# Three buffers for normalised x1 and a new order of the query part in a one-core transformer layer

## The reference, cut to what matters

```python
# attention (per batch and head)
Phi_Q = jnp.exp(-C_Q / temperature)          # C_Q: squared distances of queries to landmarks
out_unnorm = jnp.einsum('bhnk,bhkd->bhnd', Phi_Q, Y)
norm = jnp.einsum('bhnk,bhko->bhno', Phi_Q, jnp.linalg.solve(W_kernel, Phi_K_sum))
out = out_unnorm / jnp.maximum(norm, 1e-10)
...
x = _layernorm(x + attention @ Wo.T + bo)
# experts
gate_logits = xf @ Wg.T + bg
topk_vals, topk_idx = jax.lax.top_k(gate_logits, TOP_K)
gate_w = jax.nn.softmax(topk_vals, axis=-1)
...
x = _layernorm(x + experts(x))
```

## Time and profile before

| what | value |
|---|---|
| median of 3 runs | 1957.33 us (1950.88 to 1958.08) |
| the profiled execution | 1951.19 us, span 1949.4 us |
| PE busy | 1436.2 us, 74% of the span |
| DVE busy | 1244.2 us, 64% |
| ACT busy | 976.8 us, 50% |
| POOL busy | 854.8 us, 44% |
| mean granted TensorE clock | 0.871 of full speed |

### The profile page before, as it was taken

One profiled execution on the slowest core, in us unless ns is written; L12 is line 12 of the kernel. 1 busy time (PEld: TensorE's weight loads), 2 busy tenths in 40 slices (PEclk: granted clock), 3 DMA queues, 4 the chain that ended last, 5 costly groups with the idle time before them and its releaser, 6 DMA issues.

```text
span 1949.4 us, 47647 instructions
## 1 busy us (share of the span) xinstructions
PE 1436.2 (74%) x17888; PEld 1138.6 (58%) x17888; DVE 1244.2 (64%) x3410; ACT 976.8 (50%) x1699; POOL 854.8 (44%) x937
## 2 busy tenths in 40 slices
PE   4578989989897887777787888776549988894000
PEld 3267778877785555545565555554339888884000
DVE  5768854798534767767766767575646555552765
ACT  2246666766665755555555555554314333332444
POOL 2300000000001465656656566665467777777544
PEclk9689989999999998888879888889759999998555
DMA  2586786767963343434323333332427766664998
GB/s 87 93 175 143 165 191 152 174 159 172 188 145 104 96 132 108 136 107 139 123 97 112 107 112 117 111 109 91 138 85 221 224 205 212 207 213 133 362 373 298
DMA packets 255998, 307.83 MB, mean 158 GB/s; under 512 B 64896, under 2 KB 187008, under 8 KB 255360
## 3 DMA queue, kind: packets, MB, share of 16 engines
q1 hardware_dynamic: 230240, 234.49, 45.1%
q0 software_dynamic: 25536, 70.31, 9.9%
HBM read 150.02 MB, written 96.50 MB: 126 GB/s over the span
## 4 chain that ended last, share of the span: by engine, by line
PE 23%; DVE 21%; POOL 21%; issue 14%; DMA 12%; SPq 4%; ACT 3%; DVEq 0%; POOLq 0%; ACTq 0%
POOL rows_dram L658 10%; POOL terms_dram L677 6%; DMA rows_dram<-x,place_i 4%; PE bank L346 4%; PE bank L347 3%; PE bank L348 3%; POOL attn_l L642 3%; PE bank L1619 3%; DMA out<-phi 2%; PE bank L1635 2%; DVE st L1285 2%; DVE x L1277 2%; PE bank L1620 2%; DMA tile_in<-terms_dram 2%; DVE inversion L1109 2%
## 5 line engine op out<-in xcount | busy, mean ns | idle before, releaser
L658 POOL DMA_INDIRECT rows_dram<-x,place_i x256 | 283.0, 1106 | 181.3 <-DVE place_i L1346 117.2
L635 POOL TENSOR_TENSOR xl<-x_raw,xh 128x512 fp32r<-128x512 f32 x60 | 75.7, 1288 | 548.9 <-ACT xh L892 548.3
L745 ACT ACTIVATE phi<-bank,invt 128x512 f32<-128x512 f32 x256 | 162.5, 684 | 104.5 <-PE bank L1620 104.3
L868 ACT ACTIVATE phi<-bank,nlt,invt 128x512 f32<-128x512 f32 x256 | 181.3, 776 | 49.2 <-PE bank L1780 46.9
L346 PE MATMUL bank<-weh,kh 128*128 x528 | 161.9, 307 | 29.0 <-DVE kl L1429 28.7
L1619 PE MATMUL bank<-l_hh,k_hl 128*128 128x256 f32 x512 | 145.0, 315 | 40.7 <-DMA k_hl<-kl 27.1
L1429 DVE TENSOR_TENSOR kl<-bank,kh 128x512 fp32r<-128x512 f32 x132 | 90.9, 689 | 126.8 <-ACT kh L941 125.5
L1081 DVE TENSOR_SCALAR phi<-phi,phi_max,phi_min 128x1024 f32<-128x1024 f32 x128 | 103.7, 810 | 102.7 <-ACT phi L745 102.5
L1234 DVE TENSOR_SCALAR phi<-phi,phi_max,phi_min 128x1024 f32<-128x1024 f32 x128 | 111.9, 913 | 84.0 <-ACT phi L868 83.7
L346 PE MATMUL bank<-xh,wh 128*128 128x512 f32 x260 | 120.4, 463 | 51.6 <-DVE x L1277 36.4
L348 PE MATMUL bank<-wel,kh 128*128 x528 | 149.7, 284 | 0.0
(11 more groups left out here) (262 smaller groups left out, 4550.9 us busy)
## 6 DMA issues: line engine op xcount, KB each, us to landing
tile_in<-rows_dram SPq DMA_DIRECT2D x264, 130.0 KB
x_raw<-in_xT SPq DMA_DIRECT2D x64, 512.0 KB, 4.0
x_tok<-in_x SPq DMA_DIRECT2D x32, 512.0 KB, 4.8
attn<-den_dram SPq DMA_DIRECT2D x64, 256.0 KB
phi<-terms_dram SPq DMA_DIRECT2D x22, 512.0 KB, 5.6
out<-phi SPq DMA_DIRECT2D x22, 512.0 KB, 7.7
tile_in<-terms_dram SPq DMA_DIRECT2D x17, 512.0 KB, 7.0
k_hl<-attn_h SPq DMA_DIRECT2D x32, 256.0 KB
```

The source lines that it names most:

```text
L658: nc.gpsimd.indirect_dma_start(out=rows_dram, out_offset=bass.IndirectOffsetOnAxis(ap=place_i[:, at:at + 1].bitcast(u32), axis=0), in_=x1[ ...
L745: nc.scalar.activation(phi[:, n], bank[6 + s][:], ACT.Exp, scale=invt[:]).then_inc(exp_done, 1)
L868: nc.scalar.activation(phi[:, i], bank[4 + i % 4][:], ACT.Exp, bias=nlt[:, c // CPB, i:i + 1], scale=invt[:]).then_inc(qexp_done, 1)
```

## The change

Buffers: x1 gets three buffers, `place_i` two. The second set of query halves (`q_h1`, `q_l1`) no longer has memory of its own; it lies where the key and value projections' weights lay (`wh[:, 0:2]`, `wl[:, 0:2]`), which the query part does not read. The waits on `scattered` reach one chunk further back. Order: the calls in the loops of all five engines stand in another order, partly with another chunk index.

```diff
-FIRST_WEIGHTS = 2
+FIRST_WEIGHTS, X1 = 2, 3
...
-        x1 = [sb(f"x1_{i}", [P, TPC, ROW]) for i in range(2)]
+        x1 = [sb(f"x1_{i}", [P, TPC, ROW]) for i in range(X1)]
-                                 sb("place_i", [P, 2 * TPC], i32))
+                                 sb("place_i", [P, 2, 2 * TPC], i32))
-        q_h, q_l, q_sq = ([kh[0], sb("q_h1", [P, KC, CH], f32r)], [kl[0], sb("q_l1", [P, KC, CH], f32r)],
-                          [sq, sb("q_sq1", [P, KC, CH])])
+        used_up = [a[:, 0:2].rearrange("p w k n -> p (w k n)").rearrange("p (k n) -> p k n", k=KC) for a in (wh, wl)]
+        q_h, q_l, q_sq = [kh[0], used_up[0]], [kl[0], used_up[1]], [sq, sb("q_sq1", [P, KC, CH])]
```

SyncE:

```diff
-                if a - 1 > 0:
-                    load_rows(a - 1)
+                store_inverses(a + 1)
+                spread_inverses(a + 1)
+                if n > 0:
+                    load_query_x(n + 2)
+                if a + 1 > 0:
+                    load_rows(a + 1)
...
-                store_inverses(a)
-                spread_inverses(a)
-                if n - 1 > 0:
-                    load_query_x(n + 1)
```

GpSimd:

```diff
-                attn_lo(a - 1, 0)
-                attn_lo(a - 1, 1)
-                scatter(p - 1, 2)
-                scatter(p - 1, 3)
-                if n - 1 > 0:
-                    split_lo(n, 1)
-                ln1(c)
-                scatter(p, 0)
-                scatter(p, 1)
+                scatter(p, 2)
+                if n > 0:
+                    split_lo(n + 1, 1)
+                ln1(c + 1)
+                scatter(p, 3)
+                scatter(p + 1, 0)
+                attn_lo(a + 1, 0)
+                attn_lo(a + 1, 1)
+                scatter(p + 1, 1)
```

ScalarE:

```diff
-                save_attention(q - 1, 0)
-                q_exps(q, range(2, 4))
-                save_logits(p)
-                gate_exp(p)
-                q_exps(q, range(4, 6))
-                q_exps(q, range(6, 8))
+                normalise_rows(c, c % X1)
                 queries(n, 0)
-                save_attention(q - 1, 1)
                 queries(n, 1)
                 attn_hi(a, 0)
...
                 x1_copy(p + 1, 0)
                 x1_copy(p + 1, 1)
                 q_exps(q + 1, range(0, 2))
+                save_attention(q, 0)
+                q_exps(q + 1, range(2, 4))
+                if n > 0:
+                    query_hi(n + 1, 1)
+                save_logits(p + 1)
+                save_attention(q, 1)
+                q_exps(q + 1, range(4, 6))
+                gate_exp(p + 1)
+                if begins_batch(q + 2):
+                    z_landmark_major((q + 2) // CPB)
+                q_exps(q + 1, range(6, 8))
```

VectorE, the two waits and the order:

```diff
-                if c >= 2:
-                    dve.wait_ge(scattered[at], 16 * 2 * TPC * (c // 2))
+                if c >= X1:
+                    dve.wait_ge(scattered[at], 16 * 2 * TPC * (c // X1))
...
-                if p:
-                    dve.wait_ge(scattered[(p - 1) % 2], 16 * 2 * TPC * ((p - 1) // 2 + 1))
-                V.tensor_copy(place_i[:], place[:]).then_inc(place_ready, 1)
+                if p >= 2:
+                    dve.wait_ge(scattered[(p - 2) % X1], 16 * 2 * TPC * ((p - 2) // X1 + 1))
+                V.tensor_copy(place_i[:, p % 2], place[:]).then_inc(place_ready, 1)
...
                 choices(p)
+                normalise_rows(c, c % X1)
+                q_clamp(q, range(2, 4))
                 gates_end(p)
                 find_places(p)
-                q_clamp(q, range(2, 4))
                 q_clamp(q, range(4, 6))
+                normalise(a, 0)
                 q_clamp(q, range(6, 8))
-                normalise_rows(c, c % 2)
-                normalise(a, 0)
                 normalise(a, 1)
```

TensorE:

```diff
-                pe.wait_ge(den_read, min(p + 3, NCH))
+                if absent(p + 2):
+                    pe.wait_ge(ranks_read, p)
+                else:
+                    pe.wait_ge(den_read, p + 3)
...
+                denominators(q - 1, 0)
+                query_dists(q, 0)
+                denominators(q - 1, 1)
+                attention(q - 1, 0)
+                x1_transposes(p, 0)
+                x1_transposes(p, 1)
+                output_projection(c, 0)
+                output_projection(c, 1)
+                attention(q - 1, 1)
+                gate_logits(p)
+                logit_transpose(p)
                 query_dists(q, 1)
-                logit_transpose(p)
-                attention(q - 1, 1)
                 queries(n, 0)
+                if begins_batch(q + 1):
+                    z_transposes((q + 1) // CPB)
+                if begins_batch(q + 1):
+                    landmark_solve((q + 1) // CPB)
                 ranks(p)
                 queries(n, 1)
...
```

More of the change, by code:

```diff
@@ L268, in program @@
             sem("chosen_ready"), sem("ranks_done"), sem("ranks_read"), sem("place_ready"),
-            [sem(f"scattered{i}") for i in range(2)])
+            [sem(f"scattered{i}") for i in range(X1)])
         spares_stored, pad_loaded = sem("spares_stored"), sem("pad_loaded")
@@ L520, in load_tiles @@
                     chunks = ROWS_OF[min(s, len(ROWS_OF) - 1)] + 1
-                    for i in range(2):
-                        sp.wait_ge(scattered[i], 16 * 2 * TPC * (chunks // 2))
+                    for i in range(X1):
+                        sp.wait_ge(scattered[i], 16 * 2 * TPC * len(range(i, chunks, X1)))
                     if s == len(ROWS_OF):
@@ L658, in scatter @@
                     nc.gpsimd.indirect_dma_start(
-                        out=rows_dram, out_offset=bass.IndirectOffsetOnAxis(ap=place_i[:, at:at + 1].bitcast(u32), axis=0),
-                        in_=x1[p % 2][:, t], in_offset=None).then_inc(scattered[p % 2], 16)
+                        out=rows_dram, out_offset=bass.IndirectOffsetOnAxis(ap=place_i[:, p % 2, at:at + 1].bitcast(u32), axis=0),
+                        in_=x1[p % X1][:, t], in_offset=None).then_inc(scattered[p % X1], 16)
             def scatter_pads():
@@ L1323, in gates_end @@
                     return
-                aux = x1[p % 2][:, :, D:ROW]
+                aux = x1[p % X1][:, :, D:ROW]
                 dve.wait_ge(ge_ready, p + 1)
@@ L1808, in x1_transposes @@
                         at = 256 * (t % 2) + 128 * k
-                        last = nc.tensor.transpose(bank[tp][:, at:at + P], x1[p % 2][:, t, k * P:(k + 1) * P], ident)
+                        last = nc.tensor.transpose(bank[tp][:, at:at + P], x1[p % X1][:, t, k * P:(k + 1) * P], ident)
                 last.then_inc(x1t_done, 1)
```

26 lines of the change are left out of this document (4 added, 22 removed).

## The result

The changed kernel takes 1796.61 us (median of 4 runs, 1787.85 to 1798.79). The kernel before took 1954.11 us beside it (4 runs, 1950.53 to 1958.08). The ratio is 0.9185, 95% interval 0.9147 to 0.9223. The profiled execution of after took 1796.29 us, its span is 1794.1 us; before 1951.19 and 1949.4, so the spans differ by 155.3.

The account below looks back on a forecast made before the run. A ring of waits through scatter landings bound query chunks at 25.1 us; 31 chunks at 19.2 us plus extras of 28, 17, 10 and 14, less 3, gave 661 instead of 778, so 1837 us, range 1803 to 1892.

Parts of the forecast that it names:

- Ring A: POOL and DVE in one query chunk, from ln1 round to ln1 in the new order: 19.22 us, binding an ordinary chunk.
- PE's two new waits: Output projection waiting for x1_copy, 1.2 us, and logit_transpose for save_logits, 0.5, added to PE's 16.4 us of work.
- Ring D: Not forecast: DVE from residual's second half to both, then PE from ranks to the output projection's end; 17.7 us in after.
- the first pair 3.02: Ring A's term for POOL's first scatter pair, 3.02 us, taken as still stretched by the clamps beside it.
- two more pairs 5.21: Ring A's term for the two scatter pairs on POOL behind attn_lo, 5.21 us.
- less than my sum: Rival, chance 0.13: scatter pairs no longer stretched gives 1812 us, most extras absorbed 1798, both 1773.
- the extras: Time beyond ordinary chunks: plans 28 us, batch starts 17, expert weights 10, lower clock 14; 69 in all.
- the clock's 14: PE falling to the lower clock after stops at plans, batch starts and weights: 1 us at each of 14 places.
- Rival 1: DVE and POOL block one another in each chunk, normalise slipping behind attn_lo: 1877 to 1893 us; chance 0.22.
- The weighed rule: Port held by whichever instruction began first; DVE instructions with two SBUF inputs are also hit by GpSimd ones reading SBUF.
- Rival 3: The kernel gets slower, PE running the query part at the lower clock: 2038 us at 0.6 share; chance 0.04.
- Rival 4: The wait only moves: find_places or residual still waits for late scatters, 1940 to 1960 us; chance 0.05.

Follow-up runs that it names:

- e1: The kernel before in its old order with all buffers of after and their waits; 1983.91 us, ratio 0.964 to before.
- e13: The kernel of e1 run once more, beside a control; 1986.19 us, ratio 0.964 to before.
- e3: e2 with two x1 buffers instead of three; 2057.51 us, ratio 0.996 to before.
- e2: The changed kernel with the last scatter pair moved back ahead of split_lo and ln1, three x1 buffers; 2023.12 us, ratio 0.981 to before.
- the four controls: The changed kernel itself, unaltered, run again beside the experiments on other chips; ratios 0.934, 0.934, 0.935 and 0.934 to before.
- e4: The changed kernel with one place_i, so find_places waits for the scatters of the chunk before; 1962.54 us, ratio 0.954 to before.
- c1: The changed kernel itself, unaltered, as control for the runs that shorten PE and POOL; 1914.15 us, ratio 0.934 to before.

## Why the prediction was wrong

- *The wait that goes.* Right, shown: no DMA releases `residual`, the buffers alone (e1, e13) take it away and give 3.6%, and with two buffers (e3 against e2) it is back and costs 34 us.
- *Which rings are left.* Ring A as laid out is the period on the first chip, by its trace: every term stands there in the forecast order, without slack, with one idle time where it was forecast. No experiment on that chip shortened it. PE's two new waits are there, 1.24 us together instead of 1.7. Ring D was missing from the list; it is 0.7 us shorter than ring A and changes the number only on the other chips.
- *The step that failed* is the size of two terms of ring A, "the first pair 3.02 (stretched by the clamps beside it, which stay beside it)" and "two more pairs 5.21": they measured 2.64 and 4.87. Together with `gates_end` that is 0.8 us a chunk, 25 us in all, and that alone moves the sum from 1837 to 1812, inside the range. Both terms were misread from the rows of before. More of POOL's rows in before, two from the chunk of the earlier trace rows and two from the next one:

```profile
1012.38 1.06 POOL L658 DMA_INDIRECT rows_dram<-x,place_i  x1 [0.30 <-issue]
1020.56 1.36 POOL L658 DMA_INDIRECT rows_dram<-x,place_i  x1 [0.30 <-issue]
1043.37 0.98 POOL L658 DMA_INDIRECT rows_dram<-x,place_i  x1 [0.17 <-issue]
1047.25 0.96 POOL L658 DMA_INDIRECT rows_dram<-x,place_i  x1 [0.30 <-issue]
```

  The 3.02 run to the start of a third scatter and hold the 0.31 us of idle time ahead of it; the pair itself ends at 1013.44, after 2.71 (the median over chunks 1 to 29 is 2.72, in after 2.61). In the new order `attn_lo` follows, which starts 0.03 us behind the pair (0.02 behind a scatter before, at 1016.59). So some 0.3 of the 0.38 is that idle time, and 0.1 is shorter transfers. The 5.21 come from one chunk with a transfer of 1.36 us (at 1020.56); the next chunk's two pairs take 4.87 from 1043.37 on, and the median of the chunks that keep `split_lo` is 4.88 in before and 4.87 in after. The scatters' mean fell only from 1113 to 1062 ns (647 to 1425 us in before, 654 to 1273 in after). So the number came near the first half of the rival "less than my sum", which had 0.13, while its reason, scatters no longer stretched, gives only some 0.1 of the 0.7.
- *The second term that failed* is the extras, 69 against 52. Of the forecast without the clock's 14, 28 + 17 + 10 = 55, the 52 are near, and by kind as well: above 18.35 the plans' intervals without weights have 2.6, 2.9, 5.2 and 5.3 us (forecast 4), the batch starts without weights 0.2 to 3.5 (forecast 2.5), and the three plan intervals with weights 6.1 to 8.9. The lower clock did follow some of the stops:

```profile
756.00:765.00 9.00, 8.23 (x57) 6.46 (x59) 6.68 (x37) 6.20 (x11) 5.08 (x7) 0.50 0.26 90
```

  but the clock stood at 0.95 over the chunk stage, and what it cost is inside the 52 and can't be told apart there. In the number the two halves of that rival came together, 1812 less 17, against 1773 had the extras been absorbed as far as it had them.
- *Costed at nothing, and not nothing:* the ramp, 7 us. The first `residual` starts at 653.7 instead of 646.6, with the clock at 0.81 instead of 0.93 in that stage. Which call of the new order delays it wasn't tried, and the 7 are not firm: on the other chips it starts at 650.1 to 655.1 in the four controls and at 649.9 and 651.9 in e1 and e13, which have the old order.
- *Rival 1*, DVE and POOL blocking one another in each chunk (0.22), didn't come: `normalise` takes 0.68 in every chunk and never runs beside `attn_lo`. The block does exist at four of the seven plans, where the plan's last instruction takes 2.9 us, and at two of them the clamp behind it as well:

```profile
997.96 2.94 DVE L1376 COPY tile_e<-found 128x32 f32<-128x32 f32 x1
998.05 3.39 DVE L1234 TENSOR_SCALAR phi<-phi,phi_max,phi_min 128x1024 f32<-128x1024 f32 x1
```

  beside the `split_lo` of 2.52 us that POOL began at 998.34, as in the earlier trace rows. These four plans take 8.0 us, the other three 4.6 to 5.2 (before 10.0 in the earlier trace rows); without weights the chunk interval is 23.6 with the block and 20.9 and 21.2 without it, so the block costs some 2.5 us at each of the four, inside the 3 to 8 that the forecast gave a plan. The weighed rule's other half, an instruction with two SBUF inputs, can be seen in before, where the first one of `landmarks_of_batch` stood beside `attn_lo` at all six places where it ran between two chunks:

```profile
989.11 2.49 DVE L1225 TENSOR_TENSOR lm_h<-l2h,cst 128x256 fp32r<-128x256 f32 x1
```

  In after it meets no POOL tensor instruction and takes 0.36, while `residual`, with one input in PSUM, took 0.42 beside `split_lo` in before.
- *Rival 3*, the lower clock: the clock rose from 0.87 to 0.95. *Rival 4*, the wait only moves: not with two `place_i`; e4 shows it with one.
- *The signs.* The releaser of `residual` and the clock came as forecast. The ordinary chunks were shorter than the 19 to 20 us named, the intervals at plans ran from 20.9 to 27.3 and those at batch starts from 18.5 to 21.8 where 22 to 25 had been named, and POOL was busy for 451 of 619 us, 73% and not over 75.

The range failed because two parts of the sum were mis-sized in the same direction: the rival's halves had been priced at 1812 and 1798 alone and 1773 together, and the lower edge was set at 1803, between the first two.

## What to carry to other kernels

When a buffer's wait is taken away, list every cycle through the engines, those that alternate between two engines as well as those of one, and price each from rows; here three lay within 0.8 us of each other by the first chip's trace (18.4, 17.7, and PE's own 16.4 + 1.24 = 17.6), and on the other chips, where waits of 1.5 to 1.9 us come into one of them, shortening another gave nothing. Read a term from the start of its first instruction to the end of its last, not to the start of what follows: idle time ahead of the next call belongs to that call, and another call may stand there in the new order. And take it from the median of many chunks; one chunk gave 5.21 where the median was 4.88. A block by a neighbouring engine is priced by what stands beside it in the new order.

## What the runs showed of the hardware that was not expected

On the five other chips the kernel before took 5% more (2051 to 2064 us instead of 1954) and the changed kernel 6.5 to 7% more (1914 to 1925 instead of 1797), at about the same granted clock (the changed kernel 0.887 to 0.894, against 0.899). In the controls the 31 chunks take 629 to 633 us instead of 619, and what lies behind the last `residual`, nearly all of it the expert part, 625 to 636 instead of 521. The span of c1 is 115 us longer than that of after, and 106 of them lie there. The controls have waits like that of c1 above, whose releaser the trace doesn't know: 81 to 124 us of them from 600 to 1560 us, 20 to 26 of these ahead of `residual` in the chunks, and none in before and after. Most last 1.7 or about 2.5 us. What they are stays open, and so does how much of the difference they explain. They matter for reading: a change's ratio was 0.9185 on the first chip and 0.934 or 0.935 on four others, with disjoint intervals, so a ratio holds for the chip it was measured on.
